# Row sums from the operation that makes the row, squares from ScalarE, in the node and final stages of a graph network kernel

## The reference, cut to what matters

```
def _layernorm(x, g, b):                      # after each of the three attention layers
    mu = x.mean(-1, keepdims=True)
    var = ((x - mu) ** 2).mean(-1, keepdims=True)
    return (x - mu) / jnp.sqrt(var + LN_EPS) * g + b
...
for i, (...) in enumerate(layers):
    h_new = _layernorm(_gat_conv(h, src, dst, W, a_s, a_d, b, heads, concat), g, be)
    if i > 0:
        h_new = h_new + h
    h = jax.nn.relu(h_new)
...
x = x + gnn(xn) + mix(xn)
x = x + experts(_layernorm(x))
```

## Time and profile before

| | us |
|---|---|
| median of 3 runs (7530.8 to 7540.61) | 7531.67 |
| the profiled execution's own time | 7531.31 |
| its span in the profile | 7529.6 |
| node stage 1, tiles in steady work (2310 to 2426) | 116 |
| node stage 2, the same (4568 to 4706) | 138 |
| final stage, first weighing to the last reciprocal of the second norm (6854 to 7074) | 220 |
| VectorE busy in the whole span | 5498.7 (73%) |
| ScalarE busy in the whole span | 2138.7 (28%) |

### The profile page before, as it was taken

One profiled execution on the slowest core, in us unless ns is written; L12 is line 12 of the kernel. 1 busy time (PEld: TensorE's weight loads), 2 busy tenths in 40 slices (PEclk: granted clock), 3 DMA queues, 4 the chain that ended last, 5 costly groups with the idle time before them and its releaser, 6 DMA issues. The chain is left out here.

```text
span 7529.6 us, 113108 instructions
## 1 busy us (share of the span) xinstructions
PE 5390.2 (72%) x23828; PEld 3495.0 (46%) x23829; DVE 5498.7 (73%) x16160; ACT 2138.7 (28%) x5415; POOL 5176.0 (69%) x5471
## 2 busy tenths in 40 slices
PE   5677777766775677777766666587777876673399
PEld 3344444444443345444544444355555544342398
DVE  6677777777777677777777778677787777778643
ACT  2112121211113233333321113234343421113466
POOL 1777777777774777777777773777777777772444
PEclk8777787877778777777777777678888877776599
DMA  6445455544443444444444444444444444444444
GB/s 211 138 141 145 141 146 141 144 135 140 136 134 116 117 121 123 121 123 122 122 114 111 111 110 139 115 123 128 126 128 125 127 118 111 111 111 139 146 70 64
DMA packets 531615, 949.93 MB, mean 126 GB/s; under 512 B 117850, under 2 KB 366049, under 8 KB 531030
## 3 DMA queue, kind: packets, MB, share of 16 engines
q0 software_dynamic: 259808, 691.84, 34.5%
q1 hardware_dynamic: 254610, 235.89, 10.2%
q10 hardware_dynamic: 16612, 15.96, 0.6%
HBM read 796.92 MB, written 151.73 MB: 126 GB/s over the span
## 5 line engine op out<-in xcount | busy, mean ns | idle before, releaser
L1250 POOL DMA_INDIRECT edges_G<-rows,edges_index x4980 | 4749.4, 954 | 1554.4 <-issue 1481.0
L1450 PE MATMUL edges_ps_o<-edges_G,edges_OH 128*128 128x264 f32 x9960 | 3507.1, 490 | 307.1 <-DVE edges_G L1726 173.9
L1450 PEld LDWEIGHTS edges_ps_o<-edges_G,edges_OH 128*128 128x128 f32 x9960 | 2119.1, 234 | 1127.4 <-issue 634.9
L1744 DVE TENSOR_TENSOR acc<-acc,edges_ps_o 128x264 f32 x2490 | 1048.8, 421 | 821.7 <-PE edges_ps_o L1450 547.6
L1726 DVE TENSOR_TENSOR edges_G<-edges_G,edges_ps_c 128x1024 f32<-128x1024 f32 x1245 | 1500.3, 1205 | 1.8 <-ACT edges_G L1270 1.3
L1294 ACT ACTIVATE edges_OHT<-edges_ps_far 128x512 bf16<-128x512 f32 x1245 | 742.5, 596 | 1331.2 <-PE edges_ps_far L1410 1330.8
L1418 PE MATMUL edges_ps_s<-ident,edges_alpha 128*128 128x128 f32 x249 | 114.4, 459 | 1266.5 <-DVE edges_alpha L1620 1266.5
L1718 DVE TENSOR_TENSOR edges_OH<-edges_ps_c,relT 128x512 f32<-128x512 f32 x1245 | 848.6, 682 | 0.1
L1602 DVE COPY edges_node<-terms 128x12 bf16 x2490 | 476.1, 198 | 292.1 <-issue 73.8
L1418 PEld LDWEIGHTS edges_ps_s<-ident,edges_alpha 128*128 128x128 f32 x249 | 44.2, 177 | 1375.3 <-DVE edges_alpha L1620 1375.3
L1410 PE MATMUL edges_ps_far<-edges_rels,pole_rows 5*128 5x512 bf16 x1245 | 608.4, 489 | 41.3 <-DMA WT<-in_L_mix_b 19.8
(11 more groups left out here) (377 smaller groups left out, 6211.3 us busy)
## 6 DMA issues: line engine op xcount, KB each, us to landing
edges_G<-rows,edges_index POOLq DMA_INDIRECT x4980
xslot<-edges_blank SPq DMA_DIRECT2D x80, 650.0 KB
edges_masks<-lanes_of SPq DMA_DIRECT2D x123, 192.0 KB
rows<-node_ext SPq DMA_DIRECT2D x147, 130.0 KB, 2.2
experts_X<-xslot SPq DMA_DIRECT2D x105, 130.0 KB, 2.1
node_rows<-rows SPq DMA_DIRECT2D x98, 130.0 KB
h<-node_Hn SPq DMA_DIRECT2D x98, 128.0 KB, 1.7
W<-in_L_ffn_W SPq DMA_DIRECT2D x16, 512.0 KB
```

The source lines that it names most:

```text
L1250: g.indirect_dma_start(G[n][:, s, 0:RW], None, dr["rows"], bass.IndirectOffsetOnAxis(index[n][:, s:s + 1], 0)).then_inc(gathered[n], 16)
L1450: mm = pe.matmul(ps_o[BANK_OF[g]][:, 0:GW], OH[:, 2 * g + j, :], G[n][:, 2 * g + j, :], start=(j == 0), stop=(j == 1))
L1744: v.tensor_tensor(a, a, ps_o[BANK_OF[g]][:, 0:GW], ALU.add).then_inc(added, 1)
```

## The change

In node stages 1 and 2 and in the final stage VectorE's two statistics operations go. The operation that writes the row also gives its sum over the row (`accum_out`), and it is a scalar_tensor_tensor with the factor 1.0 where a plain addition stood. ScalarE takes the row with Square, bias = the sum and scale = -256, and accumulates over the row, which makes 256 squared times 256 times the variance, and then the square root as before, with the factor in its scale. Between Square and the square root ScalarE waits for its own result. VectorE gains one tiny operation a tile, the mean from the sum. In the second norm of the final stage the mean goes into the shift, so no operation is added there. Node stage 0 keeps the old form.

With fewer operations in a turn of the final stage there are four rounds for six, and the batch takes one step after a round and two after the next, so that there are again six.

```diff
@@ node_phase, vector: gather_in
-                    ch.add(v.tensor_tensor(oh, oh, a, ALU.add))
-                    yield
-                    ch.wait()
-                ch.add(v.bn_stats(stats[:, slot, :], o))
-                yield
-                wait_apart(v, chain1, ch.base + ch.n, passed)
+                    v.scalar_tensor_tensor(out=oh, in0=oh, scalar=1.0, in1=a, op0=ALU.mult, op1=ALU.add,
+                                           accum_out=total[:, slot, :]).then_inc(stats_ready, 1)
+                    return
+                v.bn_stats(stats[:, slot, :], o).then_inc(chain1, 1)
+                yield
+                wait_apart(v, chain1, b + 1, passed)
                 v.bn_aggr(mv[:, slot, :], stats[:, slot, :]).then_inc(stats_ready, 1)
@@ node_phase, vector: finish
+                if not first:
+                    v.wait_ge(stats_ready, b + 1)
+                    ch.add(v.tensor_scalar(mv[:, slot, 0:1], total[:, slot, :], 1.0 / C, None, ALU.mult))
                 v.wait_ge(sd_ready, b + 1)
@@ node_phase, scalar: std
+                a.activation(square[:, :], O[:, slot, :], ACT.Square, bias=total[:, slot, :], scale=-float(C),
+                             accum_out=mv[:, slot, 1:2]).then_inc(squared, 1)
+                a.wait_ge(squared, b + 1)
+                a.activation(sd[:, slot, :], mv[:, slot, 1:2], ACT.Sqrt, bias=eps[:, :], scale=1.0 / C ** 3).then_inc(sd_ready, 1)
@@ final_phase, vector: gather
-                c1.add(v.tensor_tensor(oh, oh, a, ALU.add))
-                yield
-                c1.wait()
-                c1.add(v.bn_stats(stats[:, slot, :], o))
-                yield
-                c1.wait()
-                v.bn_aggr(mv[:, slot, :], stats[:, slot, :]).then_inc(stats_ready, 1)
+                v.scalar_tensor_tensor(out=oh, in0=oh, scalar=1.0, in1=a, op0=ALU.mult, op1=ALU.add,
+                                       accum_out=total1[:, slot, :]).then_inc(stats_ready, 1)
@@ final_phase, vector: finish
+                v.wait_ge(stats_ready, b + 1)
+                c2.add(v.tensor_scalar(mv[:, slot, 0:1], total1[:, slot, :], 1.0 / C, None, ALU.mult))
                 v.wait_ge(sd_ready, b + 1)
...
-                v.scalar_tensor_tensor(out=hn, in0=o, scalar=0.0, in1=mix[:, slot, :], op0=ALU.max, op1=ALU.add).then_inc(x2_ready, 1)
-                yield
-                v.wait_ge(x2_ready, b + 1)
-                c2.add(v.bn_stats(stats2[:, slot, :], hn))
-                yield
-                c2.wait()
-                v.bn_aggr(mv2[:, slot, :], stats2[:, slot, :]).then_inc(stats2_ready, 1)
+                v.scalar_tensor_tensor(out=hn, in0=o, scalar=0.0, in1=mix[:, slot, :], op0=ALU.max, op1=ALU.add,
+                                       accum_out=total2[:, slot, :]).then_inc(x2_ready, 1)
@@ final_phase, vector: second
-                for _ in range(3):
-                    yield
+                yield
                 v.wait_ge(sd2_ready, b + 1)
...
-                v.tensor_scalar(shift2[:, slot, :], mv2[:, slot, 0:1], scale2[:, slot, :], -1.0, ALU.mult, ALU.mult
+                v.tensor_scalar(shift2[:, slot, :], total2[:, slot, :], scale2[:, slot, :], -1.0 / C, ALU.mult, ALU.mult
@@ final_phase, vector: the turns
-                for _ in zip_longest(*turns):
-                    next(batches, None)
+                for turn, _ in enumerate(zip_longest(*turns)):
+                    for _ in range(1 + turn % 2):
+                        next(batches, None)
@@ final_phase, scalar: std2 (std likewise, with total1, O and squared)
-                a.wait_ge(stats2_ready, b + 1)
-                a.activation(sd2[:, slot, :], mv2[:, slot, 1:2], ACT.Sqrt, bias=eps2[:, :], scale=1.0 + LN_EPS).then_inc(sd2_ready, 1)
+                a.wait_ge(x2_ready, b + 1)
+                a.activation(square[:, :], Hn[:, slot, :], ACT.Square, bias=total2[:, slot, :], scale=-float(C),
+                             accum_out=mv2[:, slot, 1:2]).then_inc(squared2, 1)
+                a.wait_ge(squared2, b + 1)
+                a.activation(sd2[:, slot, :], mv2[:, slot, 1:2], ACT.Sqrt, bias=eps2[:, :], scale=(1.0 + LN_EPS) / C ** 3).then_inc(sd2_ready, 1)
```

More of the change, by code:

```diff
@@ L583, in node_phase @@
         ext = ph.sb("ext", [P, TILE_RING, RW])
-        stats = ph.sb("stats", [P, TILE_RING, 6])
+        stats = ph.sb("stats", [P, TILE_RING, 6]) if first else None
+        total = ph.sb("total", [P, TILE_RING, 1])
+        square = ph.sb("square", [P, C])
         mv = ph.sb("mv", [P, TILE_RING, 2])
@@ L619, in node_phase @@
         owned = ph.sem("owned")
+        squared = ph.sem("squared")
         h_out = [ph.sem(f"h_out{k}") for k in range(TILE_RING)]
@@ L743, in _ @@
                 v.wait_ge(vecs_in, 32)
-            N1 = 1 if first else 2
-            N2 = 1 if first else 2 + (layer >= 2)
+            N2 = 1 if first else 3 + (layer >= 2)
             def gather_in(i, slot, last):
                 b = TILE_RING * i + slot
-                ch = Chain(v, chain1, b * N1)
                 if first:
@@ L759, in gather_in @@
                     v.wait_ge(owned, 2 * b + 2)
-                    ch.add(v.tensor_tensor(oh, oh, a, ALU.add))
-                    yield
-                    ch.wait()
-                ch.add(v.bn_stats(stats[:, slot, :], o))
+                    v.scalar_tensor_tensor(out=oh, in0=oh, scalar=1.0, in1=a, op0=ALU.mult, op1=ALU.add,
+                                           accum_out=total[:, slot, :]).then_inc(stats_ready, 1)
+                    return
+                v.bn_stats(stats[:, slot, :], o).then_inc(chain1, 1)
                 yield
-                wait_apart(v, chain1, ch.base + ch.n, passed)
+                wait_apart(v, chain1, b + 1, passed)
                 v.bn_aggr(mv[:, slot, :], stats[:, slot, :]).then_inc(stats_ready, 1)
-                assert ch.n == N1
             def finish(i, slot, last):
@@ L852, in std @@
                 a.wait_ge(stats_ready, b + 1)
-                a.activation(sd[:, slot, :], mv[:, slot, 1:2], ACT.Sqrt, bias=eps[:, :]).then_inc(sd_ready, 1)
+                if first:
+                    a.activation(sd[:, slot, :], mv[:, slot, 1:2], ACT.Sqrt, bias=eps[:, :]).then_inc(sd_ready, 1)
+                    return
+                a.activation(square[:, :], O[:, slot, :], ACT.Square, bias=total[:, slot, :], scale=-float(C),
+                             accum_out=mv[:, slot, 1:2]).then_inc(squared, 1)
+                a.wait_ge(squared, b + 1)
+                a.activation(sd[:, slot, :], mv[:, slot, 1:2], ACT.Sqrt, bias=eps[:, :], scale=1.0 / C ** 3).then_inc(sd_ready, 1)
             std(0, 0)
@@ L2010, in final_phase @@
         Hn = ph.sb("Hn", [P, TILE_RING, C])
-        stats = ph.sb("stats", [P, TILE_RING, 6])
+        total1 = ph.sb("total1", [P, TILE_RING, 1])
+        total2 = ph.sb("total2", [P, TILE_RING, 1])
+        square = ph.sb("square", [P, C])
         mv = ph.sb("mv", [P, TILE_RING, 2])
@@ L2014, in final_phase @@
         rstd = ph.sb("rstd", [P, TILE_RING, 1])
-        stats2 = ph.sb("stats2", [P, TILE_RING, 6])
         mv2 = ph.sb("mv2", [P, TILE_RING, 2])
@@ L2080, in final_phase @@
         x2_ready = ph.sem("x2_ready")
-        stats2_ready = ph.sem("stats2_ready")
+        squared = ph.sem("squared")
+        squared2 = ph.sem("squared2")
         sd2_ready = ph.sem("sd2_ready")
@@ L2409, in std @@
                 a.wait_ge(stats_ready, b + 1)
-                a.activation(sd[:, slot, :], mv[:, slot, 1:2], ACT.Sqrt, bias=eps[:, :]).then_inc(sd_ready, 1)
+                a.activation(square[:, :], O[:, slot, :], ACT.Square, bias=total1[:, slot, :], scale=-float(C),
+                             accum_out=mv[:, slot, 1:2]).then_inc(squared, 1)
+                a.wait_ge(squared, b + 1)
+                a.activation(sd[:, slot, :], mv[:, slot, 1:2], ACT.Sqrt, bias=eps[:, :], scale=1.0 / C ** 3).then_inc(sd_ready, 1)
             def std2(b):
                 slot = b % TILE_RING
-                a.wait_ge(stats2_ready, b + 1)
-                a.activation(sd2[:, slot, :], mv2[:, slot, 1:2], ACT.Sqrt, bias=eps2[:, :], scale=1.0 + LN_EPS).then_inc(sd2_ready, 1)
+                a.wait_ge(x2_ready, b + 1)
[3 more added lines that the diff above has]
+                a.activation(sd2[:, slot, :], mv2[:, slot, 1:2], ACT.Sqrt, bias=eps2[:, :], scale=(1.0 + LN_EPS) / C ** 3).then_inc(sd2_ready, 1)
             def centre(b):
```

## The result

The changed kernel takes 7564.44 us (median of five runs, 7563.84 to 7569.71) against 7530.88 for the kernel before (five runs, 7529.39 to 7540.61). The ratio is 1.0045, with a 95% interval of 1.0033 to 1.0057: slower by 34 us, 25 to 43, where +5 was forecast. The time is 2 us above the range's upper end. The profiled execution has a span of 7562.7 us.

The account below looks back on a forecast made before the run. A ring of waits was taken to bound node stage 1, with VectorE's list counting in node stage 2 and bounding the final stage. Node stages +10 and final stage -5 on 7531.3 gave 7536 us, range 7508 to 7562.

Parts of the forecast that it names:

- The bound of the node stages: Node stages: a two-tile ring of waits through TensorE, ScalarE and VectorE bounds stage 1; in stage 2 VectorE's list counts too.
- Square: Node stages: Square ahead of the root adds 0.65 us to the ring, bounds 0.46 and 0.8.
- The saving behind the reciprocal: Node stage 1: from reciprocal to row's end takes 1.4 us for 1.77, 0.37 saved.
- The step that failed: Node stages: a slower ring idles TensorE and its clock (0.91 and 0.70) may follow; left to the range's upper end.
- Final stage, VectorE's list: Final stage: VectorE loses net 0.65 us a turn with batch steps, 3.55 for 4.2 us; 31 turns give -20 us.
- Final stage, loads: Final stage: load waits behind an expert's 1 MB grow, +8 us; loads bound ten starting turns, which gain only 2.5 us.
- Final stage, logits: Final stage: six turns before a batch's logits gain nothing, and the 14.9 us of waits stay.
- Final stage, exponential: Final stage: Squares plus two table loads at each exponential stall VectorE 2 us, five times: +10 us.
- (b): Rival, faster: sum and accumulator cost nothing, ScalarE's order absorbs the Squares; node stages 0, final stage -22, 7509 us; chance 0.22.
- (c): Rival, slower: ScalarE becomes the bound, Square with read and wait 0.8 us or more; 7557 us; chance 0.19.
- (d): Rival, slower: the accumulating operation reads its rows at half rate, in node and final stages; 7565 us; chance 0.08.
- (e): Rival, slower by far: Square lies in another table than Sqrt, two loads for each of 196 Squares; 8030 us; chance 0.03.

Follow-up runs that it names:

- e1: New form in the inner node stages, old final stage of the kernel before: 7559.67 us, ratio 1.0057 to the kernel before.
- e2: New form in the final stage, old node stages of the kernel before: 7515.23 us, ratio 0.9997 to the kernel before.
- e3: Changed kernel with Square and root ahead of the copies of an earlier projection in ScalarE's list, node stages 1 and 2: 7488.98 us, ratio 0.9959.
- e4: Kernel before with the root ahead of the copies of an earlier projection in ScalarE's list, node stages 1 and 2: 7496.17 us, ratio 0.9972.
- e7: New final stage with six slots instead of TILE_RING, old node stages: 7499.02 us, ratio 0.9970 to the kernel before.
- e8: Kernel before with six slots instead of TILE_RING in the final stage: 7515.79 us, ratio 0.9995.
- e6: e1 with two unread transposes added behind each tile's projection in node stages 1 and 2: 7523.36 us, ratio 1.0002 to the kernel before.
- e11: Changed kernel, Square and root early (node stage 0: root alone), six final-stage slots, one unread transpose a tile in node stages 1 and 2: 7458.13 us, ratio 0.9918.

## Why the prediction was wrong

The forecast was +5 us: +10 in the node stages, -5 in the final stage. Measured were +39 and -1 in the profiles of before and after, and +30 in the node stages of e1 against those of e2.

- *The bound of the node stages* was read rightly: a ring, and not VectorE's busy time. e3 and e4 show it, since a change of order alone opens it. In node stage 2 the reading was only half right. The two turns that were read, with a granted clock of 0.79 and 1.00 between row and root, gave 2.75 and 2.34 us a tile, below the 2.82 that were measured, and VectorE's list was taken to count as well; the mean over 41 tiles is 5.77 us, 2.88 a tile, so the ring alone makes the stage.
- *Square* was put at 0.65 us on the ring: 0.63 measured, of which 0.51 is the operation. *The saving behind the reciprocal* was put at 0.37: 0.32 measured, 0.42 with TensorE filled. Half their difference times 49 was the forecast of +7 for node stage 1, and +3 stood for node stage 2; with the clock held, 6.4 and 6.2 were measured. These terms hold, with a miss of 3 in node stage 2.
- *The step that failed* is the last sentence of the node stages: "A slower ring also leaves TensorE idler, and the clock, which was 0.91 and 0.70, may follow; that is in the upper end." The clock did follow, to 0.80 and 0.58, and it had no term in the sum, nor as much room in the range. The row's way through TensorE was kept at the length that it had, and it is a part of the ring: 2.63 us became 3.17, and 3.26 became 3.73 in node stage 2, which is (0.54 + 0.47) x 49 / 2 = 25 us in the profiles of before and after. By the pairs with and without filling this term measures 17 to 26 us, more than the 12.6 of the operations themselves. The earlier trace rows had the hint, the same matmuls in two stages of one kernel, at 0.91 and 0.70 and 80 and 105 us busy.
- *Final stage, VectorE's list.* It lost 29 us of busy time over the stage (196.8 to 167.7), 0.6 us a tile, as put (0.65), and a turn without batch steps fell from 3.63 to some 3.0. But a turn with batch steps, waits for loads and logits taken off, fell from 4.21 to 3.83 us (means of 30 turns) and not to 3.55. Without its waits for the root, which have a term of their own below, it is 3.71: the -20 us of this term were some -15. 2.7 us of the 30 turns went to short waits of VectorE for a result just before, its own or TensorE's, of which the old form had none; the rest stays open.
- *Final stage, loads.* The waits were to grow by some 10 us (8, and 2.5 at the start) and grew by 24.8: VectorE waited for them 26 times instead of 7, and not only behind an expert's 1 MB. From the end of x2 to a gather that had to wait for the loads behind it passed 3.5 to 9.8 us, 4.6 in the median, where 3.3 to 3.6 had been put. This is the second term that was too small, and e7 shows that it held most of the gain back.
- *Final stage, logits.* "No gain" was wrong in the good direction: 14.9 fell to 9.4, counted alike. Why was not tried. A tile's time that is spent in waits for loads gives the way to the logits time to catch up, and in e7, without these waits, it is 23.6 (21.2 in e8, the old form without waits for loads); that fits, and is no proof.
- *Final stage, exponential.* A stall of 2 us five times, 10 us, was expected behind the table loads. VectorE's wait for L2426 is 4.1 us in the seven times of the stage's body, with 1.1 as the longest, and 1.0 us before: too dear by more than half, which covered a part of the miss in the loads.
- *The rivals.* (b), faster, stood on sum and accumulator at no cost: the accumulator is indeed hidden (below), and ScalarE's order doesn't absorb the Squares. (c) named a Square of 0.75 us or more and came out near the right time, 7557, by luck and for a wrong reason: Square with its read and wait is 0.63 and not 0.8, and ScalarE isn't the bound in any stage (93 of 135 us and 158 of 216). (d), the accumulating form at half rate, is refuted by the rows: 409 and 417 ns against 407 without accumulator, where it had 0.25 us more. (e), two tables, is refuted by one load of 1283 ns for a node stage.

A cause that a clock falls was not among the rivals with a chance of its own, though it was named among what would make the forecast wrong. That is what a reader should do otherwise: the thing that would break the sum belongs in it, with a price.

## What to carry to other kernels

Where a ring of waits runs through TensorE, what is added to it must be priced twice: by its own length and by the clock that TensorE loses when the same matmuls are spread over a longer stage (here it fell from 0.91 to 0.80 and from 0.69 to 0.58, and 12.6 us of the first brought 17 to 26 of the second), and one looks first whether the new operation needs to stand in the ring at all: its place in the engine's list was worth 0.86% of the time (ratio 1.0045 to 0.9959), its kind next to nothing once the place was right. Work that is taken from a full engine pays only as far as the next thing allows: ask how long a load is under way against the new, shorter turn, and give the ring of slots another turn or two with the same edit (here 1 to 7 us became 18).

## What the runs showed of the hardware

- A sum that comes with an operation of VectorE costs a DVE_READ_ACCUMULATOR of 79 to 82 ns, which begins where the next operation begins (both at 6981.22 in the timeline above, and so in 48 of the 49 of node stage 1): it takes hardly anything of the list. On ScalarE the read takes 186 to 201 ns, and the root stands behind it: Square ends at 2364.33 in the timeline of node stage 1, the read at 2364.42, and the root begins at 2364.45.
- Extra work on TensorE shortened a stage: two unread transposes a tile lifted the granted clock from 0.79 to 0.95 and from 0.61 to 0.95 (1 is full speed), and took 15.4 and 20.3 us off (e6 against e1, one execution each). In e11, with the ring open, one a tile lifted it from 0.90 to 0.95 and from 0.80 to 0.88 and took nothing off.
- Square over 16 columns takes 308 ns and over 256 columns 510. By these two it is 0.84 ns a column beside a fixed part of 0.3 us, so a Square of few columns is no way out of a ring.
